# Feed forward's operands in storage of their own, the third pair's remainder first in its step, and first and last batches' work in another order

## The reference

```python
h = _layernorm(x, ln1_g, ln1_b)
x = _attention(h, h, sa_wq, sa_wk, sa_wv, sa_wo, sa_bo) + x
h = _layernorm(x, ln2_g, ln2_b)
x = _attention(h, cond_emb, ca_wq, ca_wk, ca_wv, ca_wo, ca_bo) + x
h = _layernorm(x, ln3_g, ln3_b)
p = h @ ff_w1 + ff_b1
a, gate = (p[..., :D_FF], p[..., D_FF:])
h = a * jax.nn.gelu(gate, approximate=False) @ ff_w2 + ff_b2
return h + x
```

## Time and profile before

| | |
|---|---|
| median of 3 runs | 2836.69 us (2835.15 to 2837.28) |
| profiled execution, its own time | 2836.61 us |
| span in the profile | 2834.8 us |
| PE busy | 2809.7 us (99%), 25278 matrix products |
| DVE, ACT, POOL busy | 80%, 67%, 52% |
| chain that ended last | PE 94%, DVE 3%, POOL 2%, ACT 1% |

### The profile page before, as it was taken

One profiled execution on the slowest core, in us unless ns is written; L12 is line 12 of the kernel. 1 busy time (PEld: TensorE's weight loads), 2 busy tenths in 40 slices (PEclk: granted clock), 3 DMA queues, 4 the chain that ended last, 5 costly groups with the idle time before them and its releaser, 6 DMA issues.

```text
span 2834.8 us, 72539 instructions
## 1 busy us (share of the span) xinstructions
PE 2809.7 (99%) x25278; PEld 2512.7 (89%) x25278; DVE 2266.4 (80%) x3495; ACT 1913.5 (67%) x6041; POOL 1461.8 (52%) x1310
## 2 busy tenths in 40 slices
PE   7999999999999999999999999999999999999999
PEld 6888888888888888888888888888888889999999
DVE  6888888888888888888989889988999855555554
ACT  6777777777777777877777777777777744444443
POOL 5444444444444444755555555555555545544554
PEclk9999999999999999999999999999999999999999
DMA  6666666666666666767777776666666632222222
GB/s 151 151 163 164 160 159 157 160 153 155 150 151 150 153 152 155 171 172 176 178 177 175 175 176 169 168 164 167 170 165 163 153 101 74 74 79 86 76 74 64
DMA packets 355329, 413.33 MB, mean 146 GB/s; under 512 B 122016, under 2 KB 209440, under 8 KB 355232
## 3 DMA queue, kind: packets, MB, share of 16 engines
q1 hardware_dynamic: 345088, 395.29, 57.2%
q10 hardware_dynamic: 10144, 16.78, 1.9%
HBM read 94.52 MB, written 49.02 MB: 51 GB/s over the span
## 4 chain that ended last, share of the span: by engine, by line
PE 94%; DVE 3%; POOL 2%; ACT 1%; issue 0%; DMA 0%; ACTq 0%; DVEq 0%; POOLq 0%
PE unit_ps L612 52%; PE unit_ps L637 15%; PE s_ps L625 14%; PE s_ps L612 13%; POOL probs L1325 1%; DVE neg_max L1075 1%; DVE blocks L1089 1%; POOL w_lo L1320 0%; DVE qk_lo L1100 0%; DVE hT_lo L1113 0%; ACT probs L884 0%; DVE hT L1070 0%; ACT x_n L861 0%; DMA x_ln<-in_x_dram 0%; DVE w_lo L1041 0%
## 5 line engine op out<-in xcount | busy, mean ns | idle before, releaser
L1325 POOL TENSOR_TENSOR probs<-probs,row_inv 128x1024 f32<-128x1024 f32 x512 | 969.7, 1894 | 1059.0 <-DVE row_inv L1080 1058.9
L884 ACT ACTIVATE probs<-s_ps,neg_max 128x256 f32<-128x256 f32 x2048 | 947.7, 484 | 407.4 <-DVE neg_max L1075 406.2
L1089 DVE STREAM_TRANSPOSE blocks<-probs 128x1024 f32<-128x1024 f32 x512 | 633.8, 1238 | 124.0 <-POOL probs L1325 121.3
L1075 DVE TENSOR_REDUCE neg_max<-s_ps 128x4 f32<-128x1024 f32 x512 | 614.1, 1200 | 13.5 <-PE s_ps L625 8.4
L612 PE MATMUL unit_ps<-hT_hi,w_hi 128*128 128x256 f32 x2048 | 566.2, 280 | 3.9 <-DVE hT_lo L1113 3.7
L612 PE MATMUL unit_ps<-hT_hi,w_lo 128*128 128x256 f32 x2048 | 553.8, 277 | 0.0
L612 PE MATMUL unit_ps<-hT_lo,w_hi 128*128 128x256 f32 x1792 | 495.8, 277 | 0.0
L637 PE MATMUL unit_ps<-pT,v_f 128*64 128x256 f32 x4096 | 456.6, 381 | 0.0
L884 ACT ACTIVATION_READ_ACCUMULATOR probs<-s_ps,neg_max 128x1 f32 x2048 | 440.4, 215 | 0.0
L612 PE MATMUL unit_ps<-w_hi,a_hi 128*128 128x256 f32 x1536 | 437.8, 285 | 2.2 <-POOL a_lo L1340 1.0
L612 PE MATMUL unit_ps<-w_lo,a_hi 128*128 128x256 f32 x1536 | 426.4, 278 | 0.0
(11 more groups left out here) (73 smaller groups left out, 6011.3 us busy)
## 6 DMA issues: line engine op xcount, KB each, us to landing
pT<-blocks SPq DMA_DIRECT2D x1024, 256.0 KB, 4.5
rows_t_dram<-row_blocks SPq DMA_DIRECT2D x91, 256.0 KB, 2.3
rows_in<-rows_t_dram SPq DMA_DIRECT2D x91, 256.0 KB, 4.9
x_res<-in_x_dram SPq DMA_DIRECT2D x32, 256.0 KB, 3.1
x_sa_dram<-x_out SPq DMA_DIRECT2D x32, 256.0 KB, 2.2
x_ln<-x_sa_dram ACTq DMA_DIRECT2D x32, 256.0 KB, 4.7
ctx_in<-in_ctx_dram SPq DMA_DIRECT2D x32, 256.0 KB, 4.1
x_res<-x_sa_dram SPq DMA_DIRECT2D x32, 256.0 KB, 3.4
```

Source lines behind the costliest of these rows:

```text
L884: op = nc.scalar.activation(probs[:, m % 2, r, :].rearrange("p (j b c) -> p j b c", j=IT, c=BLK), scored.rearrange("p (j c b) -> p j b c", ...
L1075: nc.vector.tensor_reduce(neg_max[:, m % RING, :], s_ps[:, m % 2, :, :].rearrange("p h (i j) -> p (h i) j", j=S), AX_X, ALU.max, negate=Tr ...
L1089: nc.vector.transpose(blocks[:, n % 2, :, m % 2, :].rearrange("p b (j r c) -> p r j b c", j=IT, c=BLK), probs[:, m % 2, :, :].rearrange("p ...
L1325: nc.gpsimd.tensor_tensor(probs[:, m % 2, :, :], probs[:, m % 2, :, :], row_inv[:, m % RING, :].unsqueeze(2).broadcast_to([P, ROWS, S]), A ...
```

## The change

Four things, in words:

1. In the feed forward, rows and hidden values (both parts) now lie inside `pT`, the second weight in the storage of `qk_hi`/`qk_lo` (which become one tile `qk`, 512 bytes longer, so that what is allocated behind it moves by 512), and the first weight's remainder in `w_lo`, 128 bytes further on. Modulo 512 the addresses are now: rows 320, first weight 128 (rounded) and 256 (remainder), hidden values 64, second weight 384.
2. At step 0 DVE makes the third pair's remainder ahead of the reciprocal of the sums, and `scores` waits for its own pair's remainder alone.
3. The first batch: ACT loads Exp's table at once; the value projection `("v", 0, 1)` is in step 2 rather than 1; piece 5 is split by ACT ahead of the exponentials of step 1 and by POOL at step 0, behind piece 4.
4. The last batch: ACT splits the first weight's first half ahead of pair 6's exponentials and the second half behind those of pair 7, and loads Gelu's table there; DVE makes the first half's remainder early, POOL the second half's; PE transposes the feed forward's first rows ahead of the last attended values and makes the third of these before the output projection.

```diff
@@ units_of and constants
+SHIFTED_W1, SHIFTED_W2, SHIFTED_ROWS = 32, 80, 16
-LAST_ATTENDED = (0, 3, 0, 3)
+LAST_ATTENDED = (0, 3, 2, 3)
-    early = [(("v", 0, 0), "cur"), (("v", 0, 1), "cur")]
+    early = [(("v", 0, 0), "cur")]
@@ storage
-        qk_hi = sb("qk_hi", [P, RING, 2, S], F32R)
-        qk_lo = sb("qk_lo", [P, RING, 2, S], F32R)
+        qk = sb("qk", [P, 4 * RING * S + SHIFTED_W2 + 48], F32R)
+        qk_hi = qk[:, 0:2 * RING * S].rearrange("p (r a s) -> p r a s", r=RING, a=2)
+        qk_lo = qk[:, 2 * RING * S:4 * RING * S].rearrange("p (r a s) -> p r a s", r=RING, a=2)
+        transposed = pT[:].rearrange("p n j u x -> p (n j u x)").bitcast(F32R)
+        rows_hi_at, rows_lo_at = SHIFTED_ROWS, SHIFTED_ROWS + 2 * DK * S
+        hid_hi_at = rows_lo_at + 2 * DK * S + 64
+        hid_lo_at = hid_hi_at + FT * S
...
+        ff_w1_lo = w_lo[:].rearrange("p s n -> p (s n)")[:, SHIFTED_W1:SHIFTED_W1 + DK * WCOLS].rearrange(
+            "p (k n) -> p k n", k=DK)
+        ff_w2_hi = qk[:, SHIFTED_W2:SHIFTED_W2 + WCOLS]
+        ff_w2_lo = qk[:, SHIFTED_W2 + WCOLS:SHIFTED_W2 + 2 * WCOLS]
@@ weight pieces
-            return placed(t, n, {(-1, 3): [1], (0, 0): [3]}, {})
+            return placed(t, n, {(-1, 3): [1], (0, 0): [3], (0, 1): [5]}, {})
...
@@ PE scores, hidden, down
-                if m % 2 == 0:
-                    pe.wait_ge(at.qk_lo, g + 2)
+                pe.wait_ge(at.qk_lo, g + 1)
-                                   [term for k in range(DK) for term in three(w_hi[:, k, cols], w_lo[:, k, cols],
-                                                                              hT_hi[:, parity, k, :], hT_lo[:, parity, k, :])])
+                                   [term for k in range(DK) for term in three(w_hi[:, k, cols], ff_w1_lo[:, k, cols],
+                                                                              ff_rows_hi[:, parity, k, :],
+                                                                              ff_rows_lo[:, parity, k, :])])
-                    last = product(bank[:, 0:D], three(a_hi[:, m, rows], a_lo[:, m, rows],
-                                                       w_hi[:, 2, m * D:(m + 1) * D], w_lo[:, 2, m * D:(m + 1) * D]),
+                    last = product(bank[:, 0:D], three(hid_hi[:, m, rows], hid_lo[:, m, rows],
+                                                       ff_w2_hi[:, m * D:(m + 1) * D], ff_w2_lo[:, m * D:(m + 1) * D]),
@@ ACT, last batch and first
+                    if n == 3 and parts == LAST:
+                        act.wait_ge(at.qk_full, TOTAL * PAIRS)
+                        split_ff_weight(0)
...
+                        split_ff_weight(1)
+                        nc.scalar.activation(table[:], neg_half[:], ACT.Gelu)
                         attended_hi(t, 0)
-                        attended_hi(t, 1)
...
+            act.wait_ge(const_ready, 1)
+            nc.scalar.activation(table[:], neg_half[:], ACT.Exp)
@@ DVE
+                    if n == 0 and "prv" in parts:
+                        qk_remainders(t, 2)
                     if "cur" in parts:
                         invert_sums(t, 2 * n)
+                    if n == 3 and parts == LAST:
+                        split_ff_weight(0)
```

65 lines of the change are left out of this document (33 added, 32 removed).

## The result

The changed kernel takes 2841.32 us (median of 14 runs, 2840.49 to 2842.34) where the kernel before takes 2836.74 (14 runs, 2833.97 to 2837.28) on the same chip: a ratio of 1.0018, 95% interval 1.0011 to 1.0026. That is 4.6 us slower, a little less than the 0.2% (5.7 us) under which I wanted to call it no change. I had forecast 2815, within 2810 to 2821.

What follows compares the result with a forecast made beforehand. PE was taken as the bound, busy 99%, so only its product pitch and its waits at the start and between stages could pay. 11.5 + 5.7 + 1.0 + 3.6 = 21.8 us off 2836.6 gave 2815 us, own range 2810 to 2821.

Steps and rivals of the forecast that it cites:

- the third pair's remainder: Attention, step 0 on DVE: moving it ahead of the reciprocal is hidden by PE's work and removes waits, -1.0 us.
- my rivals: Whole kernel: addresses don't matter, 2826 (0.17); slow level stays, 2836.5 (0.19); new distances cost more, 2851 (0.07).
- the one on the other side: Feed forward, the slower rival: distances 320 and 448 cost more than the slow level, 2851 us; chance 0.07.
- The feed forward: PE's product pitch there: turns between two levels vanish and the fast level stays, -11.5 us.
- the distance of 0: From down to hidden, next stationary and present moving operand at equal address modulo 512: said to turn PE's pitch level.
- My bound for the new distances: Feed forward's hidden: distance 448 at one product in three might cost 10 ns each, +10 us at most.
- The start: First batch, four waits of PE touched: -5.7 us (-3 to -9).
- The table: First batch on ACT: Exp's table loaded at once, while ACT has nothing to do, -1.3 us.
- the own pair's 0.6: Start: scores(0, 0) waiting for one remainder rather than two, -0.6 us (0 to -0.8).
- piece 5 alone: Start: its earlier remainder brings the second batch's first projection to 44.7 from 48.47, -3.8 us.
- Between the stages: From attention to feed forward: hidden stops waiting for the rows' remainder, starting at 2286.3 rather than 2289.9, -3.6 us.
- walked with the old durations: Start and stage border: new order timed with profiled durations; at the border the last block transpose was put 0.7 later.

Runs made afterwards that it cites:

- the base: The changed kernel with only the third pair's remainder put back behind the reciprocal, scores still waiting for their own pair alone: 2824.32 us, ratio 0.996 to the kernel before.

## Why the prediction was wrong

**The step that failed: the third pair's remainder.** "Elsewhere nothing waits, so the edit gives 0 there, hidden by PE's own work; a reciprocal that is 0.67 us later delays POOL, which is busy 52% of the time." I gave -1.0 (0 to -2); it measured +17.1 in the trace, and 16.6 and 17.0 by the medians of the two pairs of kernels that differ by it alone. I had named the wait that it adds and who waits for it (POOL), and stopped there. PE waited only 0.4 us in two thousand, and from that I took PE's work to be the cover. The question was what DVE waits for. It had waited 56.8 us in this stretch of cross-attention for POOL's scaling, 0.93 at the step 0 shown above. With the same look I would have seen that moving work of DVE from behind the reciprocal to ahead of it takes it out of the time in which DVE waits anyway. None of my rivals held this case either; the one on the other side was another mechanism. And even without this step the change gives 2824.3, still above my 2821, for the reasons that follow.

**The feed forward: right in sign, wrong in its reason, short in size.** I gave -11.5, at 16.3 to 16.4 us a batch; it was -6.3 in this trace and -7.3 by the storage alone, at 16.48. The reason was not the distance of 0, as the kernels with the rows at 64 and with the second weight at 128 show. The new layout is fast for a thing that I had listed and had not counted on, the 448 at one product in three. The size fell short since each border costs three products of 120 ns, 3 x 6.7 = 0.02 us an `m` or 0.16 a batch, and since two batches near the end took 16.75 and 16.95. My bound for the new distances, up to +10, was not needed; the one outcome that I had not bounded, a layout at 120 throughout, is 24 us dearer than this one.

**The start: -5.7 given, -3.8 measured, and part of that is luck.** The table is as predicted: loaded at once, off the way of the normalised rows, which start at 6.66, where the table before began to load then. ACT in the kernel after:

```profile
1.82 1.28 ACT L1035 ACT_TABLE_LOAD   x1 [1.82 <-issue]
...
6.66 1.44 ACT L878 ACTIVATE x_n<-x_ln,ln_shift,rstd 128x256 f32<-128x256 f32 x2 [3.34 <-POOL ln_shift L1326]
```

The wait of 3.17 for piece 5's remainder is gone too. But PE now waits elsewhere:

```profile
20.78 0.36 PE L628 MATMUL unit_ps<-hT_hi,w_hi 128*128 128x256 f32 x1 [0.86 <-DVE w_lo L1055]
...
28.44 0.98 PE L640 MATMUL s_ps<-qk 64*128 64x256 f32 x12 [1.39 <-ACT probs L901]
...
30.75 1.65 PE L640 MATMUL s_ps<-qk 64*128 64x256 f32 x12 [1.33 <-ACT probs L901]
...
44.22 0.36 PE L628 MATMUL unit_ps<-hT_hi,w_hi 128*128 128x256 f32 x1 [1.11 <-DVE hT_lo L1133]
```
```profile
28.44:33.80 5.36, 4.03 (x31) 3.63 (x32) 3.67 (x8) 2.36 (x10) 4.49 (x7) 0.70 0.82 186
```

The first is new: what came sooner runs into piece 2's remainder and waits 0.86, which takes back the own pair's 0.6, a term that measured nothing. The two waits for exponentials are the ones that I had walked (1.4 to 1.6). "I count no half clock behind waits of 1.4 to 1.8 us" was wrong, for the clock is at 0.70 there over 5.4 us, a mean of stretches at either level; but it cost nothing. The base kept 1.00 there, stood idle later instead, and has the second batch's first projection at 44.30, no sooner than the 44.22 here:

```profile
38.85 0.51 PE L628 MATMUL unit_ps<-w_hi,hT_hi 128*128 128x512 f32 x1 [1.35 <-DVE qk L1120]
```

I had 44.7 for piece 5 alone and about 43 with the table and the own pair. What I took for a fixed cost of the kernel before, the half clock behind piece 5's wait, belonged in part to that one execution: other traces of the same instructions reach that projection at 45.50 to 46.89 rather than 48.47. Against those, the new start gives 1.3 to 2.7 us there. By the mark of batch 1 the kernel after then loses 0.4 on the base, behind the remainder's new order: it waits 1.09 us for the next copy of the values where the base waits 0.51.

**Between the stages: -3.6 given, -2.3 measured.** `hidden` did stop waiting for the rows' remainder. What I had not costed is that DVE and POOL slow each other. DVE and POOL in the kernel after:

```profile
2287.90 2.26 DVE L1061 TENSOR_TENSOR w_lo<-w_stage,w_hi 128x2048 fp32r<-128x2048 f32 x1
2291.94 1.25 DVE L1109 STREAM_TRANSPOSE blocks<-probs 128x1024 f32<-128x1024 f32 x1 [1.79 <-POOL probs L1345]
...
2296.60 1.25 DVE L1115 TENSOR_TENSOR a_lo<-unit_ps,a_hi 128x512 fp32r<-128x512 f32 x2
2297.77 2.53 DVE L1168 TENSOR_TENSOR pT<-hT,pT 128x512 fp32r<-128x512 f32 x1
```
```profile
2288.06 3.85 POOL L1345 TENSOR_TENSOR probs<-probs,row_inv 128x1024 f32<-128x1024 f32 x1 [3.19 <-DVE row_inv L1100]
...
2295.18 4.58 POOL L1364 TENSOR_TENSOR w_lo<-w_stage,w_hi 128x2048 fp32r<-128x2048 f32 x1
```

The scaling of pair 6, 1.89 us everywhere else, takes 3.85 beside the weight's first half on DVE, and the block transpose stands 2.0 later. Later the rows' remainder on DVE takes 2.53 where the same line takes 0.69 elsewhere, beside POOL's half of the split. The Trainium skill ("SBUF — State Buffer", section "Who interferes with whom") states it: a DVE instruction with two inputs in SBUF contends with a GpSimd instruction that reads SBUF. The trace agrees, with these two numbers. The pieces that were "walked with the old durations" were exactly the pairs to which that applies. Both fit an instruction that stands until the other one's end and then takes its own time: 2290.16 + 1.89 = 2292.05, where the scaling ends at 2291.91, and 2299.76 + 0.69 = 2300.45, where the rows' remainder ends at 2300.30. PE then waits 0.95 us ahead of the attended values of step 2 where it had waited 0.8 for `a_lo` before:

```profile
2295.93 1.95 PE L652 MATMUL unit_ps<-pT,v_f 128*64 128x256 f32 x16 [0.95 <-issue]
```

The row names no releaser. What landed last ahead of it is the fourth move of pairs 4's and 5's blocks, at 2295.84, 6.7 us after its issue where the three ahead of it took 3.7 to 4.6; why it took so long is open. But that is not what sets the time. The output projection behind needs DVE's remainders `a_lo`, which stand behind the late block transpose and end at 2297.85; the projection starts at 2297.99. In the base that move landed in time, and PE waits for `a_lo` instead:

```profile
2280.78 0.35 PE L628 MATMUL unit_ps<-w_hi,a_hi 128*128 128x256 f32 x1 [0.81 <-DVE a_lo L1115]
```

In both kernels `hidden` starts 15.9 us after the first product behind the last scores, where I had 14.6 and the kernel before has 18.2. So the step that failed here is the walk with old durations, by the 2.0 of the block transpose against the 0.3 that I gave it; this is read from the times, and no kernel without that overlap was run.

**The best version.** The change with the remainder's old order is faster than both kernels, 2824.32. Its 12.1 us are the storage's 7.3, the start's 2.1 and the rest, 2.7, for the own pair's wait and the work between the stages together; these last two weren't run apart. By the marks the work between the stages gives 2.4 in the base's trace, and the own pair's wait nothing that can be told.

## What to carry to other kernels

Before work is moved ahead of an instruction that another engine waits for, look at what the moved engine itself waits for next: if that is the answer of the other engine, the work was free where it stood, and what is moved can cost its whole length in each round (here 0.57 for 0.60 us, and 1.19 for 1.2), whatever the busy shares say. The chain of work that ended last shows it afterwards better than any busy time. A term taken from one trace's half clock should be looked for in a second execution before it is counted: here it was worth up to 3 us, in the same instructions. Where two levels of a pitch are seen, a layout is found by trying several, one distance at a time; a reading drawn from one trace fits by chance.
